# A fused attention and convolution kernel: the mask products of the first scores moved ahead of the first convolution, and one more step taken into TensorE's inner loop

## The chip, the cores and the metric

The kernel runs on one core of one Trainium2 chip. The metric is the device time of one execution in microseconds (us); a program's time is the median of its runs. Before the change it is 2295.17 us, the median of 3 runs that lie between 2292.28 and 2295.76 us.

## The reference

The input is 8 images of 128 x 128 pixels with 64 channels, in float32. Every pixel attends to its 3 x 3 neighbourhood, then three 3 x 3 convolutions with ReLU follow, and a residual is added:

```python
q = x @ Q_P;  k = neighbours(x) @ K_P;  v = neighbours(x) @ V_P      # 9 neighbours of each pixel, zero outside
scores = (k . q) * mask                 # (8, 128, 128, 9)
alpha  = softmax(scores, axis=-1)
t_in   = x + sum(alpha * v)
t = relu(conv3x3(t_in, ff1) + b1)       # 64 -> 64
t = relu(conv3x3(t,    ff2) + b2)       # 64 -> 128
t = relu(conv3x3(t,    ff3) + b3)       # 128 -> 64
out = t_in + t
```

## The kernel before

**Tiling and steps.** Two images are worked on together (rows 0 to 63 and 64 to 127 of the partitions), so there are 4 pairs. A pair is cut into 16 bands of 8 rows. TensorE runs 17 steps for a pair, k = 0 to 16, 68 in all. A step computes the attention of the next band, b, and the three convolutions of bands already there; k = 15 is the one step without attention, because the next band belongs to the next pair and is fetched by k = 16. The convolutions are run as sums and differences over pairs of columns: each has four streams whose results lie in four banks (`conv_banks`), and VectorE (DVE) joins the streams again in a "middle" and an "outer" addition.

**Attention of a band.** `r_product` (L372) multiplies x by the folded query and key weights, into `mix_bank` and `proj_bank`; ScalarE (ACT) copies the result to `rq` (L639). `scores` does half of a band: four 64 x 64 products with 400 columns (L387) write the mask, 0 inside the window and a large negative number outside, into the two banks `score_banks`; then 16 products in float32, each 32 rows of two passes in the trace (L393), add the scores to it. DVE takes the maxima (`max_scores`, L756), ACT the exponentials (L627), DVE scales (`scale`, L762 and L765) to `prob`. `turn` (L405) transposes `prob` into the same `score_banks`, ACT copies it to `probt` (L644), `mix` (L420) and `v_product` (L432) finish the band, and DVE adds x (L776).

**Order on TensorE.** It is written out by hand in `step`: r_product; the inner streams of the first convolution (`conv1`, L442); the first scores; the outer streams of conv1; the four tiles of the third convolution (`conv3_tile`, L484), with turn and the second scores between them; then the second convolution (`begin2`, `go_on2`, `end2`, L500) with mix and v_product between its parts. At its beginning the inner conv1 waits until DVE has done the outer addition of the odd rows of the step before (`outer(G, k - 1, ODD, 1)`, L866), and `conv3_tile(G, k, 0)` waits until DVE has done `middle1` of this step (L832 and L833), since both use the same banks. `conv3_tile(G, k, 1)` waits for `prob` ahead of its last two taps.

**Order on DVE.** At the start of a step: outer ODD (L866), one part of the inputs of conv1 (L794), outer EVEN (L866), inputs of both halves (L789, L790; these wait for ACT's ReLU, L693), `max_scores(b, 0)` (L756), `middle1` (L832, L833), `max_scores(b, 1)`, `outer1` (L841), `scale(b, 0)`, further inputs (L794), `scale(b, 1)`.

**Loops.** TensorE runs a loop over the 4 pairs. Inside it the steps k = 0 and 1 are written out, an inner loop of 12 turns does k = 2 to 13, and k = 14, 15 and 16 are written out. The other engines have loops of their own, in which k = 14 is also written out; the change leaves those as they are. At the end of a step `await_band` waits for the next band's x and for the end of this band's attention, in all steps but k = 14.

Of the kernel before, what the change touches and what calls it, by code (L numbers as in the profile page):

```python
# [16 lines left out]
BANDS = H // BAND  # L17
# [4 lines left out]
KEYS = HALO * HALO  # L22
PATCHES = W // PATCH
GROUP = 4
# [50 lines left out]
def build(nc, x_bands, x_keys, qt2, kt, vbd, w1, w2, w3, b1, b2, b3, window, eye, eye16, out):  # L75
    with ExitStack() as ctx:
# [3 lines left out]
        def pb(name, shape):  # L80
            return ctx.enter_context(nc.psum_tensor(name, shape, F32))
# [50 lines left out]
        for slots in (2, 2, 4, 4):  # L132
            n = slots * 3 * 128
# [7 lines left out]
        score_banks = pb("score_banks", [128, 2, 512])  # L141
# [75 lines left out]
        def outer_read(G, which, behind=0):  # L217
            n = {CONV1: 2, CONV3: 4, ODD: 7, EVEN: 8}[which]
            return G * DVE_READS + (n + DVE_READS - DVE_READS * behind - (2 if G is ALL_STEPS else 0))
# [137 lines left out]
        def _(pe):  # L357
            def hold(bank):

                nc.tensor.matmul(bank[:, 0:2], eye16_sb[:], window_sb[:, 0:2], start=True, stop=True)  # L360

            def await_band(b):
                pe.wait_ge(t_ready, b * 2)
                pe.wait_ge(xc_in, b * 16 + 16)
                pe.wait_ge(xs_in, b * 32 + 32)

            def r_product(b):
                near, far = xc[:, 1:1 + BAND, 1:65], xs[:]
                for bank, band, done, swap in ((mix_bank, near, r_done[0], False), (proj_bank, far, r_done[1], True)):
                    for rows in (LOWER, UPPER):  # L370
                        to = (UPPER if rows is LOWER else LOWER) if swap else rows
                        nc.tensor.matmul(bank[to].rearrange("c (a r s) -> c a r s", r=PATCH, s=PATCH), qk[rows],  # L372
                                         band[rows].rearrange("c r (a s) -> c a r s", s=PATCH),
                                         start=True, stop=True).then_inc(done, 1)

            def await_r(b, half):
                pe.wait_ge(r_ready, b * 2 + (half + 1))
                if half:
                    pe.wait_ge(probt_ready, b * 2 + 1)

            def scores(b, half):
                banks = [score_banks[:, n, 0:GROUP * KEYS].rearrange("q (a n) -> q a n", n=KEYS) for n in range(2)]
                mask = window_sb[:].rearrange("q (o n) -> q o n", o=1).broadcast_to([128, GROUP, KEYS])
                for n, swap in ((0, False), (1, True)):
                    for rows in (LOWER, UPPER):
                        to = (UPPER if rows is LOWER else LOWER) if swap else rows
                        nc.tensor.matmul(banks[n][to], eye16_sb[rows, rows], mask[rows], start=True, stop=False)  # L387
                for a in range(GROUP):
                    for n, swap in ((0, False), (1, True)):
                        patch = half * HALF + n * GROUP + a  # L390
                        for rows in (LOWER, UPPER):
                            to = (UPPER if rows is LOWER else LOWER) if swap else rows
                            mm = nc.tensor.matmul(banks[n][to, a], rq[rows, patch],  # L393
                                                  xc[rows, :, patch * PATCH:patch * PATCH + HALO],
                                                  start=False, stop=a == GROUP - 1)
                            if a == GROUP - 1:
                                mm.then_inc(scores_done, 1)
# [26 lines left out]
            def await_y(b):  # L424
                pe.wait_ge(y_ready, b * 2 + 2)
# [22 lines left out]
            def conv1(G, k, b, outer, att=False):  # L448


                pe.wait_ge(dt_done, b * 2 - (0 if outer else 1))
                if outer:
                    pe.wait_ge(dve_read, outer_read(G, EVEN, 1))
                else:
                    pe.wait_ge(t_kept, G * 16 + 16)
                    pe.wait_ge(dve_read, outer_read(G, ODD, 1))
                streams = (0, 3) if outer else (2, 1)
                for n, m in enumerate(streams):
                    for i in range(2):
                        if att and n == 1 and i == 1:  # L460
                            await_r(b, 0)
                        for o in ((0,) if k == BANDS else (0, 1)):
                            tap1(k, i, m, n, FULL, o, 1 if k == 0 else o, n == 0, n == 1 and k == BANDS)
                for n, m in enumerate(streams):
                    for i, rows, o in ((0, LOWER, 0), (0, UPPER, 1), (1, UPPER, 0), (1, LOWER, 1)):
                        if o == 0 and k == 0:
                            tap1(k, i, m, n, FULL, o, 0, False, n == 1)
                        elif o == 1 or k < BANDS:
                            tap1(k, i, m, n, rows, o, 1 - o, n == 0 and k == BANDS, n == 1)
# [28 lines left out]
            def tap2(k, which, j, rows, s, w, d, start, stop):  # L498
                lo, hi = pairs2(k)
                return nc.tensor.matmul(conv_banks[:, bank_of(which, j), lo * 128:hi * 128],  # L500
                                        w[rows, STREAMS[j], 2 * (which == EVEN) + s],
                                        d[rows, lo + s:hi + s, STREAMS[j]], start=start, stop=stop)
# [30 lines left out]
            def end2(G, k, j, ahead=None):  # L533

                pe.wait_ge(half_done, G * 8 + (2 * j + 2))
                for n, (w, d) in enumerate(((w2h, duh), (w2l, duh), (w2h, dul))):
                    if ahead and n == 2:
                        ahead()
                    odd = tap2(k, ODD, j, LOWER, 1, w, d, False, n == 2)
                    even = tap2(k, EVEN, j, UPPER, 0, w, d, False, n == 2)  # L540
                odd.then_inc(tile_done, 1)
                even.then_inc(tile_done, 1)
# [7 lines left out]
            r_product(0)  # L550
            await_r(0, 0)
            hold(score_banks[:, 0])
            scores(0, 0)
            await_prob(0, 0)
            hold(score_banks[:, 0])
            turn(0, 0)
            await_r(0, 1)
            hold(score_banks[:, 0])
            scores(0, 1)
            mix(0, 0)  # L560
            await_prob(0, 1)
# [11 lines left out]
            def step(G, k, b, att):  # L573
                if att:
                    r_product(b)
                conv1(G, k, b, False, att)
                if att:
                    scores(b, 0)
                conv1(G, k, b, True)
                conv3_tile(G, k, 0)  # L580
                conv3_tile(G, k, 1, (lambda: await_prob(b, 0)) if att else None)
                if att:
                    turn(b, 0)
                conv3_tile(G, k, 2, (lambda: await_r(b, 1)) if att else None)
                if att:
                    scores(b, 1)
                conv3_tile(G, k, 3)
                if att:
                    mix(b, 0)
                begin2(G, k, 0)  # L590
                go_on2(G, k, 0)
                begin2(G, k, 1, (lambda: await_prob(b, 1)) if att else None)
                if att:
                    turn(b, 1)
                go_on2(G, k, 1)
                end2(G, k, 0)
                end2(G, k, 1)
                if att:
                    mix(b, 1)
                begin2(G, k, 2, (lambda: await_y(b)) if att else None)  # L600
                if att:
                    v_product(b)
                go_on2(G, k, 2)
                begin2(G, k, 3)
                go_on2(G, k, 3)
                end2(G, k, 2)
                next_band = None if k == BANDS - 2 else b if k == BANDS - 1 else b + 1
                end2(G, k, 3, None if next_band is None else lambda: await_band(next_band))

            with pe.Fori(0, PAIRS) as p:  # L610
                g0, b0 = p * STEPS, p * BANDS
                step(g0, 0, b0 + 1, True)
                step(g0 + 1, 1, b0 + 2, True)
                with pe.Fori(0, BANDS - 4) as h:
                    step(g0 + h + 2, 2, b0 + h + 3, True)
                step(g0 + (BANDS - 2), BANDS - 2, b0 + (BANDS - 1), True)
                step(g0 + (BANDS - 1), BANDS - 1, b0 + BANDS, False)
                step(g0 + BANDS, BANDS, b0 + BANDS, True)
            for j in range(4):
# [432 lines left out]
```

## Time and profile before

| | before |
|---|---|
| median of 3 runs | 2295.17 us |
| the profiled execution, whole time | 2292.98 us |
| its span, first to last instruction | 2291.0 us |
| PE busy (TensorE matmul) | 2184.0 us, 95% |
| PEld busy (TensorE weight load) | 1222.3 us, 53% |
| DVE busy | 1894.3 us, 83% |
| ACT busy | 1132.7 us, 49% |
| mean granted TensorE clock | 0.987 of full speed |

The profiled execution is 0.1% shorter than the median. Its time is the span and 2.0 us around it. A busy PE is read with care: the ends of matmuls are modelled, and a matmul's row is longer than the slot that it takes in a stream, so slots are read from start to start.

### The profile page before, as it was taken

The numbers are of one execution on the slowest core, as the hardware profiler recorded it, in microseconds if no ns is written. First come the engines' busy times: TensorE is split into PE (matmuls) and PEld (weight loads), VectorE is DVE, ScalarE is ACT, GpSimd is POOL, SyncE is SP. The second block draws the span as 40 slices with busy tenths as digits, with TensorE's granted clock in tenths as the row PEclk, the third lists the DMA queues.
The fourth block names the chain that finished last, engine by engine and source line by source line (L and its number), as shares of the span: only waits on it lengthen the run. The fifth ranks groups of instructions, "written<-read, shape, count | busy, mean of one in ns | idle before, by whom it ended". The sixth has DMA issues, their size and how long they took to land.

```text
span 2291.0 us, 63881 instructions
## 1 busy us (share of the span) xinstructions
PE 2184.0 (95%) x24401; PEld 1222.3 (53%) x24401; DVE 1894.3 (83%) x2850; ACT 1132.7 (49%) x3108; POOL 15.5 (1%) x24
## 2 busy tenths in 40 slices
PE   4999999999899999999989999999988999999998
PEld 2555555554455555555455555555545555555554
DVE  4888888888688888888768888888876888888885
ACT  2555455553455455455345555555434555554542
POOL 2000000000000000000000000000000000000000
PEclk8999999999999999999999999999999999999999
DMA  5454544554355444544345445445534544454444
GB/s 130 140 145 142 166 141 136 155 153 136 103 155 168 145 140 147 161 145 132 118 145 154 136 154 156 145 132 166 151 117 111 168 146 142 139 166 145 141 147 124
DMA packets 291284, 328.75 MB, mean 144 GB/s; under 512 B 89300, under 2 KB 223252, under 8 KB 284564
## 3 DMA queue, kind: packets, MB, share of 16 engines
q1 hardware_dynamic: 291164, 327.17, 48.2%
q8 instruction: 73, 1.20, 0.2%
q14 instruction: 47, 0.39, 0.1%
HBM read 152.50 MB, written 33.82 MB: 81 GB/s over the span
## 4 chain that ended last, share of the span: by engine, by line
PE 87%; DVE 6%; issue 3%; ACT 1%; DMA 1%; SPq 1%; DVEq 0%; ACTq 0%
PE conv_banks L484 29%; PE conv_banks L500 24%; PE conv_banks L442 17%; PE mix_bank L420 5%; PE score_banks L393 4%; DVE work L866 3%; PE score_banks L405 3%; PE mix_bank L432 3%; PE score_banks L387 1%; DMA work<-w 1%; ACT probt L644 1%; DVE prob L765 0%; PE mix_bank L372 0%; ACT prob L627 0%; DVE tf L776 0%
## 5 line engine op out<-in xcount | busy, mean ns | idle before, releaser
L484 PE MATMUL conv_banks<-dodd,w3f 128*64 128x512 f32 (+1 forms) x1656 | 503.5, 582 | 11.9 <-DVE work L833 9.2
L484 PE MATMUL conv_banks<-deven,w3f 128*64 128x512 f32 (+1 forms) x1656 | 496.3, 570 | 8.7 <-DVE prob L765 7.0
L627 ACT ACTIVATE prob<-score_banks,negmax 128x100 f32<-128x100 f32 x1040 | 343.0, 343 | 195.4 <-DVE negmax L756 195.4
L442 PE MATMUL conv_banks<-dt,w1f 128*64 128x256 f32 (+3 forms) x4224 | 413.9, 384 | 22.3 <-DVE work L866 22.3
L442 PEld LDWEIGHTS conv_banks<-dt,w1f 128*64 128x64 f32 (+1 forms) x4224 | 219.2, 135 | 235.9 <-DVE work L866 83.4
L500 PE MATMUL conv_banks<-duh,w2h 64*128 64x512 f32 (+2 forms) x1632 | 327.6, 399 | 4.0 <-ACT m_sb L663 2.1
L500 PE MATMUL conv_banks<-duh,w2l 64*128 64x512 f32 (+2 forms) x1632 | 319.3, 388 | 6.0 <-DVE prob L765 5.2
L500 PE MATMUL conv_banks<-dul,w2h 64*128 64x512 f32 (+2 forms) x1632 | 282.4, 396 | 0.9 <-DVE tf L776 0.9
L484 PEld LDWEIGHTS conv_banks<-dodd,w3f 128*64 128x64 f32 x1656 | 138.0, 137 | 236.4 <-issue 212.0
L644 ACT COPY probt<-score_banks 100x1024 f32<-100x1024 f32 x130 | 131.8, 1014 | 235.0 <-PE score_banks L405 235.0
L484 PEld LDWEIGHTS conv_banks<-deven,w3f 128*64 128x64 f32 x1656 | 155.1, 138 | 158.8 <-issue 114.6
L639 ACT COPY rq<-mix_bank 128x512 f32<-128x512 f32 x65 | 38.2, 587 | 391.1 <-PE mix_bank L372 391.1
L756 DVE TENSOR_REDUCE negmax<-score_banks 128x4 f32<-128x400 f32 x260 | 148.5, 572 | 97.1 <-PE score_banks L393 96.5
L627 ACT ACTIVATION_READ_ACCUMULATOR prob<-score_banks,negmax 128x1 f32 x1040 | 212.2, 204 | 0.0
L693 ACT ACTIVATE relued<-work,bias 128x1024 f32<-128x1024 f32 (+2 forms) x136 | 149.6, 1103 | 92.5 <-DVE work L866 92.5
L866 DVE TENSOR_TENSOR work<-conv_banks,work 128x1024 f32<-128x1024 f32 (+2 forms) x136 | 157.5, 1163 | 44.0 <-PE conv_banks L500 44.0
L500 PEld LDWEIGHTS conv_banks<-dul,w2h 64*128 64x128 f32 x1632 | 143.5, 185 | 75.2 <-issue 53.4
L663 ACT COPY m_sb<-conv_banks 128x512 f32<-128x512 f32 (+3 forms) x205 | 108.1, 562 | 146.0 <-PE conv_banks L484 107.2
L500 PEld LDWEIGHTS conv_banks<-duh,w2l 64*128 64x128 f32 x1632 | 153.6, 185 | 49.8 <-ACT rq L634 15.1
L500 PEld LDWEIGHTS conv_banks<-duh,w2h 64*128 64x128 f32 x1632 | 153.2, 184 | 47.5 <-ACT m_sb L663 3.9
L420 PEld LDWEIGHTS mix_bank<-probt,xk 100*64 100x64 f32 x4160 | 139.4, 139 | 58.0 <-issue 56.8
L806 DVE TENSOR_TENSOR dul<-work,duh 128x1024 fp32r<-128x1024 f32 (+1 forms) x136 | 159.1, 1170 | 0.0
(93 smaller groups left out, 2937.6 us busy)
## 6 DMA issues: line engine op xcount, KB each, us to landing
xk<-x_keys SPq DMA_DIRECT2D x66, 800.0 KB
xc<-x_bands SPq DMA_DIRECT2D x66, 650.0 KB, 5.0
dodd<-dodd SPq DMA_DIRECT2D x68, 512.0 KB, 5.1
xr<-x_bands SPq DMA_DIRECT2D x264, 128.0 KB, 3.5
out<-work SPq DMA_DIRECT2D x60, 512.0 KB, 2.7
dt<-dt SPq DMA_DIRECT2D x68, 256.0 KB, 2.3
deven<-deven SPq DMA_DIRECT2D x68, 256.0 KB, 5.6
duh<-duh SPq DMA_DIRECT2D x68, 256.0 KB, 2.4
```

Of the source, the lines that this page charges most:

```text
L393: mm = nc.tensor.matmul(banks[n][to, a], rq[rows, patch], xc[rows, :, patch * PATCH:patch * PATCH + HALO], start=False, stop=a == GROUP - 1)
L420: last = nc.tensor.matmul(mix_bank[image, a * C:(a + 1) * C], xk[:, patch, image], probt[:, half, i if a < GROUP else 1 - i, a], start=Tru ...
L442: mm = nc.tensor.matmul(bank[(LOWER, UPPER)[o], n * 256 + lo * 64:n * 256 + hi * 64], w1f[i][rows, m, s, o * C:o * C + C], dt[rows, lo + s ...
L484: return nc.tensor.matmul(bank[rows, lo * 128:hi * 128], w3f[:, m, s, odd * C:odd * C + C], source[:, lo + s // 2:hi + s // 2, m], start=s ...
L500: return nc.tensor.matmul(conv_banks[:, bank_of(which, j), lo * 128:hi * 128], w[rows, STREAMS[j], 2 * (which == EVEN) + s], d[rows, lo + ...
L627: last = nc.scalar.activation(prob[:, g % 2, a], score_banks[:, g % 2, a * KEYS:(a + 1) * KEYS], ACT.Exp, bias=negmax[:, g % 2, a:a + 1], ...
L644: nc.scalar.copy(probt[:, half], score_banks[0:KEYS].rearrange("n i (a q) -> n i a q", q=C)).then_inc(probt_ready, 1)
L663: nc.scalar.copy(m2_sb[:, which % 2, lo:hi], bank[:, lo:hi]).then_inc(act_read, 1)
L693: nc.scalar.activation(to[:, lo:hi, :, 1:1 + W], sums[which][:, lo:hi], ACT.Relu, bias=bias[:, 1:2]).then_inc(relu_done, 1)
L756: nc.vector.tensor_reduce(negmax[:, g % 2], score_banks[:, g % 2, 0:GROUP * KEYS].rearrange("q (a n) -> q a n", n=KEYS), AX_X, ALU.max, ne ...
L806: nc.vector.tensor_tensor(dul[:, 1:n + 1, streams], du[:, 0:n, streams], duh[:, 1:n + 1, streams].bitcast(F32), ALU.subtract).then_inc(du_ ...
L866: nc.vector.tensor_tensor(both, m03, both, ALU.add).then_inc(dve_read, 1)
```

## The change

The four mask products leave `scores` and become a function of their own, `masks`. For the second half of a band `masks()` is called right ahead of `scores(b, 1)`, where the products were. For the first half it is called between `r_product(b)` and the inner conv1; `scores(b, 0)` stays behind the inner conv1. In the work ahead of the loops `masks()` stands right ahead of both scores. The inner loop of TensorE runs 13 turns in place of 12 (k = 2 to 14), the written-out step k = 14 goes, and with it the exception by which that step didn't wait for the next band.

```diff
-            def scores(b, half):
-                banks = [score_banks[:, n, 0:GROUP * KEYS].rearrange("q (a n) -> q a n", n=KEYS) for n in range(2)]
+            banks = [score_banks[:, n, 0:GROUP * KEYS].rearrange("q (a n) -> q a n", n=KEYS) for n in range(2)]
+
+            def masks():
                 mask = window_sb[:].rearrange("q (o n) -> q o n", o=1).broadcast_to([128, GROUP, KEYS])
                 for n, swap in ((0, False), (1, True)):
                     for rows in (LOWER, UPPER):
                         to = (UPPER if rows is LOWER else LOWER) if swap else rows
                         nc.tensor.matmul(banks[n][to], eye16_sb[rows, rows], mask[rows], start=True, stop=False)
+
+            def scores(b, half):
...
             def step(G, k, b, att):
                 if att:
                     r_product(b)
+                    masks()
                 conv1(G, k, b, False, att)
                 if att:
                     scores(b, 0)
...
                 conv3_tile(G, k, 2, (lambda: await_r(b, 1)) if att else None)
                 if att:
+                    masks()
                     scores(b, 1)
...
-                next_band = None if k == BANDS - 2 else b if k == BANDS - 1 else b + 1
-                end2(G, k, 3, None if next_band is None else lambda: await_band(next_band))
+                end2(G, k, 3, lambda: await_band(b + 1 if att else b))
...
-                with pe.Fori(0, BANDS - 4) as h:
+                with pe.Fori(0, BANDS - 3) as h:
                     step(g0 + h + 2, 2, b0 + h + 3, True)
-                step(g0 + (BANDS - 2), BANDS - 2, b0 + (BANDS - 1), True)
```

## Rows read from the trace of the kernel before

**Rows 1.** The page's part 4: the chain that ended last, by engine.

```profile
PE 87%; DVE 6%; issue 3%; ACT 1%; DMA 1%; SPq 1%; DVEq 0%; ACTq 0%
```

**Rows 2.** Waits from 112.9 to 509.6 us (k = 2 to 13): us in total, times, longest.

```profile
DVE negmax L756 <- PE score_banks L393: 11.2, 12, 0.9
...
PE conv_banks L442 <- DVE work L866: 3.4, 12, 0.3
```

**Rows 3.** Window of step k = 7: length; busy PE, PEld, DVE, ACT, POOL; clock; DMA.

```profile
311.26:344.31 33.05, 32.77 (x371) 18.14 (x369) 28.85 (x42) 17.26 (x47) 0.00 (x0) 1.00 0.49 147
```

**Rows 4.** Timeline, start of step k = 7: start, us, engine, line, operation, [idle before <-releaser].

```profile
311.46 1.23 DVE L866 TENSOR_TENSOR work<-conv_banks,work 128x1024 f32<-128x1024 f32 x1 [0.58 <-PE conv_banks L500]
311.80 0.66 PE L372 MATMUL mix_bank<-xc,qk 64*64 64x512 f32 x2
...
312.74 2.97 PE L442 MATMUL conv_banks<-dt,w1f 128*64 128x256 f32 x32 [0.28 <-DVE work L866]
```

**Rows 5.** Timeline, same step: the mask products and what stands around them.

```profile
315.32 0.13 PEld L387 LDWEIGHTS score_banks<-window_sb,eye_sb 64*64 64x64 bf16 x4
...
315.54 0.35 PE L387 MATMUL score_banks<-window_sb,eye_sb 64*64 64x400 bf16 x4
...
315.70 0.87 PE L393 MATMUL score_banks<-xc,rq 64*64 64x100 f32 x32
```

**Rows 6.** Timeline, same step: DVE's maxima and middle1, and conv3's first load.

```profile
317.43 0.55 DVE L756 TENSOR_REDUCE negmax<-score_banks 128x4 f32<-128x400 f32 x1
...
318.51 0.67 DVE L833 TENSOR_TENSOR work<-conv_banks,m_sb 128x512 f32<-128x512 f32 x1
...
319.41 0.20 PEld L484 LDWEIGHTS conv_banks<-dodd,w3f 128*64 128x64 f32 x4 [0.39 <-issue]
```

**Rows 7.** Timeline, k = 15: its start, middle1, conv3's load; k = 16: the latter two.

```profile
544.12 1.08 PE L442 MATMUL conv_banks<-dt,w1f 128*64 128x256 f32 x8 [1.41 <-DVE work L866]
...
549.38 0.68 DVE L833 TENSOR_TENSOR work<-conv_banks,m_sb 128x512 f32<-128x512 f32 x1
...
550.19 0.20 PEld L484 LDWEIGHTS conv_banks<-dodd,w3f 128*64 128x64 f32 x4 [0.65 <-issue]
...
577.04 0.28 DVE L833 TENSOR_TENSOR work<-conv_banks,m_sb 128x128 f32<-128x128 f32 x1
...
577.46 0.65 PE L484 MATMUL conv_banks<-dodd,w3f 128*64 128x512 f32 x2 [2.08 <-DVE work L833]
```

**Rows 8.** Timeline, k = 7: second maxima, outer1, and the load that awaits prob.

```profile
319.11 0.55 DVE L756 TENSOR_REDUCE negmax<-score_banks 128x4 f32<-128x400 f32 x1
319.71 1.23 DVE L841 TENSOR_TENSOR work<-conv_banks,work 128x1024 f32<-128x1024 f32 x1
...
323.52 0.38 PEld L484 LDWEIGHTS conv_banks<-deven,w3f 128*64 128x64 f32 x4 [0.48 <-DVE prob L765]
```

**Rows 9.** Timeline, step k = 1: middle1, conv3's first product, outer1, the wait for prob.

```profile
89.40 0.69 DVE L833 TENSOR_TENSOR work<-conv_banks,m_sb 128x512 f32<-128x512 f32 x1
...
90.80 1.23 DVE L841 TENSOR_TENSOR work<-conv_banks,work 128x1024 f32<-128x1024 f32 x1 [0.23 <-PE conv_banks L442]
...
90.50 0.86 PE L484 MATMUL conv_banks<-dodd,w3f 128*64 128x256 f32 x5
...
94.61 0.65 PE L484 MATMUL conv_banks<-deven,w3f 128*64 128x256 f32 x4 [1.44 <-DVE prob L765]
```

**Rows 10.** Timeline, the turns from k = 13 to the written-out k = 14.

```profile
509.27 0.40 PE L500 MATMUL conv_banks<-dul,w2h 64*128 64x512 f32 x2
509.59 0.70 PE L372 MATMUL mix_bank<-xc,qk 64*64 64x512 f32 x2
```

**Rows 11.** Timeline, the turns from one pair to the next (k = 16 to k = 0).

```profile
604.00 1.12 PE L372 MATMUL mix_bank<-xc,qk 64*64 64x512 f32 x2 [3.94 <-issue]
...
1723.03 1.11 PE L372 MATMUL mix_bank<-xc,qk 64*64 64x512 f32 x2 [6.64 <-issue]
```

**Rows 12.** Window, 6.7 us from the first turn of a pair: length, busy, clock.

```profile
601.00:607.70 6.70, 3.70 (x18) 1.36 (x20) 3.90 (x9) 2.29 (x5) 0.00 (x0) 0.50 0.50 122
```

More of the change, by code:

```diff
@@ L575, in step @@
                     r_product(b)
+                    masks()
                 conv1(G, k, b, False, att)
@@ L585, in step @@
                 if att:
+                    masks()
                     scores(b, 1)
```

## The prediction

> **What bounds the kernel now.** I read the chain of waits by engine first: TensorE is 87% of it, DVE 6% [rows 1]. The DVE part has one place. In the wait table of twelve ordinary steps TensorE's matmuls idle for one thing only, conv1 behind DVE's outer addition L866, 0.28 us in each step [rows 2, 4]. The windows say the same from outside: step k = 7 lasts 33.05 us with PE busy for 32.77 [rows 3]. Then the timeline of that step's start. The last products of the step before release DVE's outer addition at 311.46, which ends at 312.69; conv1 starts at 312.74. r_product's last row ends at 312.46, so the gap is 0.28 us [rows 4]. The end of the gap is set by DVE and not by what TensorE does in it. An ordinary step is thus a ring: TensorE's end, one DVE addition of 1.23 us, TensorE again.
>
> **Moving the masks: what it takes away.** In step k = 7 the four mask products start at 315.54 and the scores at 315.70: a slot of 0.16 us in a stream without idle time [rows 5]. Without them the scores start 0.16 us after conv1's start sooner. The first score weights must then be loaded where the mask's are now, at 315.32 during conv1's last pass, 0.22 us ahead of the slot; four loads took 0.13 us together [rows 5]. That cover holds; if it didn't, at most the 0.13 us would come back.
>
> **What it adds.** The same 0.16 us goes in behind r_product. From the end of its last row to conv1 there are 0.28 us [rows 4], and that end is modelled late, so the masks fit with at least 0.12 us to spare. r_product itself doesn't move, nor does ACT's copy of it. No wait is added: the banks' last reader was ACT's copy of the turned probabilities of the step before, for which mix has already waited. If the cover were gone, conv1 would start later by what juts out and the scores sooner by the same 0.16 us; the move would be even.
>
> **What is late next.** Here the naive sum (60 steps by 0.16 us) breaks. Behind conv1 stands conv3, which waits for middle1. DVE's way there starts at the same outer addition that releases conv1: outer, inputs, outer, inputs, maxima, middle1, one behind the other, and in k = 7 it runs from 311.46 to 319.18 (318.51 and 0.67) without pause worth naming [rows 4, 6]. The maxima start at 317.43, long after the scores' last products are issued (315.70 and 0.87 end at 316.57) [rows 5, 6]: scores that come sooner don't move them. So DVE stays where it is against the step's start, and the question is how close conv3 stands behind middle1. In k = 7 its first load is at 319.41, 0.23 us after middle1's end [rows 6]. Where conv3 really waits for middle1, the load comes 0.13 us after it: in k = 15 550.06 to 550.19, in k = 16 577.32 to 577.46 for the matmul, with 2.08 us of idle time named after L833 [rows 7]. So conv3 can come forward by 0.23 - 0.13 = 0.10 us and no more; of the 0.16 us, 0.06 turn into idle time ahead of conv3. The rows' rounding leaves 0.08 to 0.12.
>
> **Behind that gate.** The next is the wait for prob in conv3's second tile: the weight load stood 0.48 us for it while the matmuls never did [rows 8]. outer1 (L841) started at 319.71, 0.05 us after the end of the maxima before it (319.11 and 0.55) [rows 8], while middle1 and the maxima overlap by 0.07 [rows 6, 8]; I read that as a wait for conv1's end, which now comes 0.16 us sooner. I take it forward by about 0.1 us, the probabilities behind it too, so they keep pace with TensorE's 0.10. If outer1 doesn't move, the load has the time from 323.52 to its matmul's turn, some 0.2 us, which 0.10 doesn't use up. At the second scores DVE waits for TensorE again, 0.9 us in each step [rows 2], and from there to the end everything moves together.
>
> **The sum over steps.** k = 2 to 14: 13 steps by 4 pairs by 0.10 us = 5.2 us (4.2 to 6.2). k = 1: conv3 starts 0.41 us after middle1 (90.09 to 90.50), so the gate leaves 0.28; later it idles 1.44 us for prob, but the chain of prob hangs on outer1, which waited 0.23 us for conv1 [rows 9]: the whole 0.16 us goes through, 4 by 0.16 = 0.6 us. k = 16: idle for middle1 already, 2.08 us [rows 7], which DVE alone sets: nothing. k = 0: conv1 doesn't wait for DVE there; the masks are only done earlier: nothing. k = 15 has none. The second scores' masks stay where they were: nothing. Sum: 5.8 us less.
>
> **One more step in the loop.** The instructions of k = 14 are those of k = 2. A turn of the inner loop costs no more than going on to written-out code: from the last product of k = 13 to k = 14's r_product there are 0.32 us [rows 10], and k = 7, reached by the loop, shows no idle time at its start either [rows 4]. The new wait for the next band in k = 14 has queued behind it the last six products and k = 15; the other ordinary steps have that wait and never idle for it [rows 2], and the loads it names are issued in k = 14 as in them. I cost both at nothing; the bound above is the next paragraph's.
>
> **The turn of the outer loop** is different. Between pairs TensorE stands 3.94 us, once 6.64, for nothing that the profile names [rows 11], and then runs at 0.50 of the clock, 1.2 GHz, for a while [rows 12]. The program of a pair becomes a step shorter, yet the jump still goes far back. I leave these three stalls as they are, and take their own difference, 6.64 - 3.94 = 2.7 us, as what can fall out either way. The Trainium skill ("Runtime: NRT & Kernel Launch", section on instruction fetch mechanics) says that a taken branch whose target isn't among the instructions held forces a fetch before execution goes on. By that rule the stall at the outer turn stays, and the trace agrees, with 3.94 us there against none at the inner one.
>
> **Against the median.** The profiled execution took 2292.98 us, the median is 2295.17; the sum shortens either alike. 2295.17 - 5.8 = 2289.4 us (for the profiled execution 2287.2). A measurement of this kernel can tell 0.2% from no change, 4.6 us, and the forecast stands only just beyond it.
>
> **The rivals.**
> - *The gate isn't there* (12%): conv3 needs no 0.13 us behind middle1, or DVE moves too. Then 56 steps give 0.16 us, 9.0 us: 2286.2 us. Against it speaks the 0.13 us of both stalled steps [rows 7].
> - *The gate takes nearly all* (24%): DVE's chain is a little longer beside the masks, or a second gate (prob, u) stands closer than its waits show, or the scores' weights lose their cover (0.13 of 0.16 us). Each would leave 0.03 us in a step at most, 52 by 0.03 = 1.6 us: 2293.6 us. For it speaks that DVE is busy for 28.85 of 33.05 us [rows 3].
> - *The move does nothing* (5%): the masks don't fit into the gap and push conv1 by all they gave: 2295.2 us. The gap's 0.28 us speak against it.
> - *The other side* (4%): the inner loop's exit now falls into other code, and if that isn't at hand TensorE stands at each of 4 exits as at the outer turn, 3.94 us, against the 1.41 us that k = 15 waits for DVE's outer addition anyway [rows 7] and the low clock after it. It decides from the point where the stall passes that wait. With 2.5 to 3.9 us by 4 and half of a 6.7 us stretch at 0.50 clock [rows 11, 12], 4 by about 6 = 24 less 5.8: some 2313 us. The exit into k = 14 without a stall speaks against it [rows 10].
>
> The three outer turns lie across all of these: each may cost 2.7 us more or less [rows 11], and two that fall out worse take the forecast to 2289.4 + 5.4 = 2294.8 us.
>
> **How the numbers follow.** The forecast, 0.10 us in an ordinary step, has 55%. Its own size goes from 4.8 to 6.8 us, and the outer turns add about 2.7 us on either side: 2285.7 to 2293. The range for 8 in 10 takes in the missing gate and most of the second rival: 2284.5 to 2295.0. Faster by over 0.2% is below 2290.6: the 12% and four fifths of the 55%, with a little of the rest, 0.58. Slower by over 0.2% are the 4% and a trifle of the turns, 0.05. The rest, 0.37, is within.
>
> **What would show it.** In an ordinary step: L387's first four between L372 and L442, conv1 0.28 us after r_product's row as before and now with the masks' row in the gap; scores 2.80 us after conv1's start in place of 2.96; the load of conv3 0.13 us after L833's end in place of 0.23, and a new wait of L484 for L833 in all steps; a step of 32.95 us. k = 16 unchanged. Wrong would be: conv1 later than 0.05 us after L866's end (masks don't fit), a step of 32.89 us (no gate), matmuls idle for L765 (the second gate), or idle time at the start of k = 15 beyond 1.4 us.

## The result, and the profile after the change

The changed kernel takes 2281.57 us, the median of 6 runs, against 2293.73 us of the kernel before (6 runs): 12.2 us or 0.5% less, a ratio of 0.9949 with a 95% interval of 0.9937 to 0.9961. A second set of five runs gave 2281.85 us. The forecast was 5.8 us less, 2289.4 us with a range of 2284.5 to 2295.0: the direction came true, the size did not, and the time lies below the range. Of the 7.8 us between forecast and result 1.4 are the starting point, since the kernel before had 2295.17 us in its first three runs and has 2293.73 in six.

The page of the changed kernel, its span, busy times and the chain by engine (answering rows 1):

```profile
span 2278.5 us, 63905 instructions
...
PE 2183.9 (96%) x24401; PEld 1226.9 (54%) x24401; DVE 1888.2 (83%) x2850; ACT 1132.8 (50%) x3108; POOL 15.5 (1%) x24
...
PE 86%; DVE 7%; issue 3%; ACT 2%; DMA 1%; SPq 1%; DVEq 0%; ACTq 0%
```

PE is as busy as before (2184.0 us), with the same 24401 matmul rows: nothing was saved in work. What went is idle time and low clock. The timeline of step k = 7, without ACT and SP (answering rows 4, 5 and 6; the masks are now L388, conv1 L445, scores L396, conv3 L487, middle1 L838):

```profile
311.65 1.23 DVE L871 TENSOR_TENSOR work<-conv_banks,work 128x1024 f32<-128x1024 f32 x1 [0.57 <-PE conv_banks L503]
...
311.99 0.66 PE L372 MATMUL mix_bank<-xc,qk 64*64 64x512 f32 x2
312.37 0.45 PE L388 MATMUL score_banks<-window_sb,eye_sb 64*64 64x400 bf16 x4
...
312.93 2.97 PE L445 MATMUL conv_banks<-dt,w1f 128*64 128x256 f32 x32
...
315.72 0.87 PE L396 MATMUL score_banks<-xc,rq 64*64 64x100 f32 x32
...
318.65 0.69 DVE L838 TENSOR_TENSOR work<-conv_banks,m_sb 128x512 f32<-128x512 f32 x1
...
319.47 0.20 PEld L487 LDWEIGHTS conv_banks<-dodd,w3f 128*64 128x64 f32 x4 [0.43 <-issue]
```

The masks stand in the gap, and conv1 starts 0.05 us after the outer addition's end as before (312.88 to 312.93). The scores follow conv1's start by 2.79 us; before it was 2.96 (312.74 to 315.70 in rows 4 and 5). Then comes the gate: conv3's first load stands 0.13 us behind middle1 (319.34 to 319.47), where it stood 0.23 [rows 6], at exactly the distance that only the waiting steps k = 15 and 16 showed before [rows 7]. In all 48 steps k = 2 to 13 this distance is 0.13 us after the change, and 0.22 to 0.25 before it. The twelve steps k = 2 to 13 of the first pair, in one window before and after (columns as in rows 3):

```profile
112.92:509.59 396.67, 393.25 (x4418) 217.62 (x4416) 346.01 (x504) 207.01 (x564) 0.00 (x0) 1.00 0.50 148
```

```profile
113.85:508.97 395.12, 393.75 (x4418) 218.51 (x4416) 344.62 (x505) 207.06 (x564) 0.00 (x0) 1.00 0.50 149
```

A step takes 32.93 us in place of 33.06. Cutting both spans at the starts of the steps, as the timelines give them, tells where all of the 12.4 us between them lie:

| part of the span | before, us | after, us | difference |
|---|---|---|---|
| up to the first k = 1 | 82.4 | 83.6 | +1.1 |
| k = 1, four steps | 121.9 | 121.2 | -0.7 |
| k = 2 to 13, 48 steps | 1586.6 | 1580.8 | -5.8 |
| k = 14, four steps | 138.2 | 137.7 | -0.5 |
| k = 15, four steps | 107.1 | 107.1 | 0.0 |
| k = 16 up to the start of k = 0, three times | 105.4 | 100.3 | -5.0 |
| k = 0, three steps | 104.5 | 104.3 | -0.2 |
| the last k = 16 and the rest | 44.8 | 43.5 | -1.3 |

k = 1 to 14 give 7.0 us. The forecast had costed k = 16 and the outer turns at nothing, and there lie 6.3 us. What happens there is seen in k = 16, from the end of its wait for middle1 to its next wait in conv2: the four pairs before the change, then the four after it (the clock is the third number from the end):

```profile
577.46:592.72 15.26, 14.48 (x150) 6.75 (x150) 10.69 (x24) 8.70 (x37) 0.00 (x0) 1.00 0.24 50
1133.39:1150.34 16.95, 16.16 (x150) 7.08 (x150) 10.77 (x24) 8.66 (x37) 0.00 (x0) 0.90 0.21 53
1692.09:1709.05 16.96, 16.17 (x151) 7.18 (x151) 10.73 (x24) 8.66 (x37) 0.00 (x0) 0.90 0.21 49
2252.68:2269.65 16.97, 16.18 (x151) 7.18 (x152) 10.75 (x24) 8.66 (x37) 0.00 (x0) 0.90 0.21 50
```

```profile
576.74:592.00 15.26, 14.48 (x151) 6.75 (x151) 10.67 (x24) 8.67 (x37) 0.00 (x0) 1.00 0.24 50
1130.41:1147.36 16.95, 16.17 (x150) 7.16 (x150) 10.73 (x24) 8.65 (x37) 0.00 (x0) 0.90 0.21 50
1686.18:1701.45 15.27, 14.48 (x151) 6.76 (x151) 10.68 (x24) 8.70 (x37) 0.00 (x0) 1.00 0.22 59
2241.54:2256.80 15.26, 14.48 (x150) 6.75 (x150) 10.65 (x24) 8.66 (x37) 0.00 (x0) 1.00 0.23 54
```

The same work takes 15.26 us at full clock, and 16.96 where the clock falls to 1.2 GHz behind the 2.1 or 2.2 us of idle time: 1.7 us for each fall. The low stretch of the second pair before the change, by itself:

```profile
1133.41:1136.81 3.40, 3.40 (x8) 0.99 (x10) 3.13 (x8) 2.20 (x14) 0.00 (x0) 0.50 0.03 7
```

There are three falls before and one after. The third outer turn was 6.64 us before [rows 11] and is 3.81 after, which is the other 2.8 us. Against these stands a slower beginning (+1.1 us). So the study has two questions: is the gate what I took it for, and are the falls of the clock an effect of the change or of chance?

### The profile page after: what moved, and what is told of

Read it like the earlier page. It is cut to its first block, busy times and chain, and to the rows that moved or that the text cites. A ratio compares the mean times of both kernels' runs of the same rounds, so it can differ in the third digit from the quotient of the medians.

```text
span 2278.5 us, 63905 instructions
## 1 busy us (share of the span) xinstructions
PE 2183.9 (96%) x24401; PEld 1226.9 (54%) x24401; DVE 1888.2 (83%) x2850; ACT 1132.8 (50%) x3108; POOL 15.5 (1%) x24
## 4 chain that ended last, share of the span: by engine, by line
PE 86%; DVE 7%; issue 3%; ACT 2%; DMA 1%; SPq 1%; DVEq 0%; ACTq 0%
PE conv_banks L487 30%; PE conv_banks L503 24%; PE conv_banks L445 16%; PE mix_bank L423 5%; PE score_banks L396 4%; DVE work L871 3%; PE score_banks L408 3%; PE mix_bank L435 3%; PE score_banks L388 1%; DMA work<-w 1%; ACT probt L649 1%; DVE prob L770 0%; DVE negmax L761 0%; ACT relued L698 0%; PE mix_bank L372 0%
## 5 line engine op out<-in xcount | busy, mean ns | idle before, releaser
L487 PE MATMUL conv_banks<-dodd,w3f 128*64 128x512 f32 (+1 forms) x1656 | 500.8, 579 | 12.6 <-DVE work L838 9.8
L487 PE MATMUL conv_banks<-deven,w3f 128*64 128x512 f32 (+1 forms) x1656 | 494.7, 568 | 8.7 <-DVE prob L770 7.0
L445 PE MATMUL conv_banks<-dt,w1f 128*64 128x256 f32 (+3 forms) x4224 | 413.4, 383 | 12.2 <-DVE work L871 5.6
L445 PEld LDWEIGHTS conv_banks<-dt,w1f 128*64 128x64 f32 (+1 forms) x4224 | 219.0, 135 | 207.2 <-issue 71.2
L487 PEld LDWEIGHTS conv_banks<-dodd,w3f 128*64 128x64 f32 x1656 | 138.9, 137 | 237.6 <-issue 212.8
L487 PEld LDWEIGHTS conv_banks<-deven,w3f 128*64 128x64 f32 x1656 | 155.8, 138 | 155.2 <-issue 111.5
L871 DVE TENSOR_TENSOR work<-conv_banks,work 128x1024 f32<-128x1024 f32 (+2 forms) x136 | 157.1, 1160 | 43.6 <-PE conv_banks L503 43.6
```

What stands on the lines that cost most here:

```text
L445: mm = nc.tensor.matmul(bank[(LOWER, UPPER)[o], n * 256 + lo * 64:n * 256 + hi * 64], w1f[i][rows, m, s, o * C:o * C + C], dt[rows, lo + s ...
L487: return nc.tensor.matmul(bank[rows, lo * 128:hi * 128], w3f[:, m, s, odd * C:odd * C + C], source[:, lo + s // 2:hi + s // 2, m], start=s ...
L871: nc.vector.tensor_tensor(both, m03, both, ALU.add).then_inc(dve_read, 1)
```

## The experiments

A fall means in what follows that the window above takes 16.6 to 17 us in place of 15.26 to 15.5. The inner work of a profile, the sum of k = 1 to 14, is called the core sum; it is 1846.7 us before and 1839.7 after. The extra products of five kernels are these; nobody reads what they write:

```python
            def fill(n):
                many = window_sb[:].rearrange("q (o n) -> q o n", o=1).broadcast_to([128, GROUP, KEYS])
                to = mix_bank[:, 0:GROUP * KEYS].rearrange("q (a n) -> q a n", n=KEYS)
                for _ in range(n):
                    nc.tensor.matmul(to, eye16_sb[:], many, start=True, stop=True)
```

### The two halves of the change, apart

The masks moved alone, against the changed kernel, with the exception of k = 14 from its wait again:

```diff
-                end2(G, k, 3, lambda: await_band(b + 1 if att else b))
+                next_band = None if k == BANDS - 2 else b if k == BANDS - 1 else b + 1
+                end2(G, k, 3, None if next_band is None else lambda: await_band(next_band))
...
-                with pe.Fori(0, BANDS - 3) as h:
+                with pe.Fori(0, BANDS - 4) as h:
                     step(g0 + h + 2, 2, b0 + h + 3, True)
+                step(g0 + (BANDS - 2), BANDS - 2, b0 + (BANDS - 1), True)
```

> Only the masks are moved; the loops are as in the kernel before. Theory A (an ordinary step gains until conv3 meets middle1, and the rest of the 12 us comes from the steps k = 16 and the outer turns, which fall as the program's times fall): an ordinary step of 32.93 us, conv3's first load 0.13 us after middle1; 7.0 us less than before from k = 1 to 14, and another 0 to 5 us by what k = 16 and the outer turns do. Rival B (the shorter program of a pair is what shortens the outer turns): 7.0 us less and no more, 2286.7 us, the third outer turn at 6.6 us again.

Measured: 2283.18 us against 2292.45, ratio 0.9956 (0.9942 to 0.9969). The core sum is 1839.6 us, as after. Two of four pairs had a fall.

The loop alone, against the kernel before, is the same edit the other way; the change of the wait isn't shown again:

```diff
-                with pe.Fori(0, BANDS - 4) as h:
+                with pe.Fori(0, BANDS - 3) as h:
                     step(g0 + h + 2, 2, b0 + h + 3, True)
-                step(g0 + (BANDS - 2), BANDS - 2, b0 + (BANDS - 1), True)
```

> Only k = 14 is taken into the inner loop; the masks stay behind the inner conv1. Theory A: ordinary steps of 33.05 us and the same gaps as before; no difference from before, 2293.7 us, or one of about 3 us by how the outer turns and the low clock happen to fall. Rival B (the shorter program shortens the outer turns): some 4 to 5 us less, 2289 us, all of it between the start of k = 16 and that of k = 0.

Measured: 2291.85 us against 2292.45, ratio 1.0001 (0.9992 to 1.0010); core sum 1846.5 us, four falls of four. The loop step is worth nothing that shows beyond 2 us, as costed, and rival B is gone: the shorter program doesn't shorten the time. The gain belongs to the masks.

The kernel before, unchanged, for a second profile:

> The kernel before, unchanged, for a second profile. If the third outer turn's 6.64 us is a property of the program, it stands there again, at the same place; if it is how loads happen to fall in one execution, it is 3.9 us or falls on another turn. Likewise the low clock in k = 16, which stood in three of four pairs. Time 2293.7 us either way.

Measured: 2293.22 us. The core sum repeats to 0.3 us (1846.4); the falls are four of four. The third outer turn is 4.85 us in place of 6.64, the first two 3.70 and 3.57. So the turn differs between executions of one program, and the 2.8 us that it seemed to give are mostly chance of the one profiled execution. The falls are another matter: seven of eight pairs in two profiles.

### The gate at middle1

```diff
-                if att:
-                    max_scores(b, 0)
                 middle1(G, k)
                 if att:
+                    max_scores(b, 0)
                     max_scores(b, 1)
```

> The changed kernel with DVE's middle1 ahead of the first maxima, so that conv3 finds middle1 done some 0.55 us sooner. Theory A (middle1 is the gate that takes 0.06 us of an ordinary step's gain): conv3's first load comes again 0.30 us after conv1's last matmul's start in place of 0.36, an ordinary step takes 32.87 us, 52 by 0.06 = 3 us less than the changed kernel, and in k = 16 up to 0.5 us of the 2.2 us wait goes: 2277 us or so. Rival C (another gate stands right behind, prob above all, since its chain now starts 0.6 us later): steps of 32.93 us or more, with matmuls idle for prob (L770).

Measured: 2278.87 us against 2292.45 (ratio 0.9949, 0.9936 to 0.9963). The timeline of k = 7, middle1 and conv3's first load:

```profile
319.64 0.68 DVE L838 TENSOR_TENSOR work<-conv_banks,m_sb 128x512 f32<-128x512 f32 x1
...
320.86 0.20 PEld L487 LDWEIGHTS conv_banks<-dodd,w3f 128*64 128x64 f32 x4 [0.39 <-issue]
```

conv3 now stands 0.54 us behind middle1 (320.32 to 320.86), and its load has the 0.39 us before it again that it had before the change [rows 6]; the changed kernel shows 0.43. The mean of the 48 steps is 32.88 us against 32.93, and the core sum 1837.1 us, 2.6 us below the changed kernel's. The wait of k = 16 is 1.77 us in place of 2.24. Theory A gave 3 us for the core and 32.87; rival C, a second gate at prob, doesn't show: with prob's chain starting later, no ordinary step has matmuls idle for it. The gate is shown, and with it the 0.05 to 0.06 us that it took of each step's 0.16: from before (33.05) to here (32.88) the mean step is shorter by the whole 0.16 or 0.17.

### Falls of the clock: place or time?

First, was it the idle time of k = 16 at all? The products fill it:

```diff
                 conv1(G, k, b, True)
+                if k == BANDS:
+                    fill(11)
                 conv3_tile(G, k, 0)
```

> The kernel before with 11 idle-time products (400 columns in bf16, into mix_bank, read by nobody) ahead of conv3 in k = 16, where TensorE otherwise stands 2.1 us for middle1. Theory A (what the change gained beyond the 7.0 us of k = 1 to 14 is low clock after that idle time, which stood in 11 of 12 pairs of three profiles with the masks behind conv1, and costs 1.7 us each): no low clock there, conv3 of k = 16 not later by more than 0.05 us, and 4 by 11/12 by 1.7 = 6 us less than before, 2286.5 us. Rival D (the low clock in k = 16 isn't it): 2292.5 us.

> The changed kernel with the same 11 products in the same place. Theory A: with moved masks the low clock stood in 4 of 12 pairs, so only 4 by 1/3 by 1.7 = 2.3 us are left to win, 2279.3 us; its distance to the kernel before with the same products is then the 7.0 us of the ordinary steps and no more. Rival D: a distance of 10 to 12 us between those two kernels, as without the products.

Measured: 2293.91 us against 2294.26 for the one (ratio 0.9993, 0.9984 to 1.0002), 2286.06 us for the other (ratio 0.9955, 0.9942 to 0.9968; five runs, a sixth took 5819.16 us, for an unknown reason, and isn't counted). Neither gains; the second is 4 us above the changed kernel. conv3 isn't late by the products, and the fall behind the wait is gone in all eight pairs; but in three pairs of the kernel before with the products it comes later and is longer. Two windows of the first pair, one behind the wait and one from there over the rest of k = 16, the turn and the first microseconds of k = 0:

```profile
577.00:594.00 17.00, 16.11 (x176) 7.78 (x176) 12.38 (x29) 9.19 (x39) 0.00 (x0) 1.00 0.29 76
594.00:612.00 18.00, 13.30 (x116) 8.60 (x114) 8.26 (x18) 4.22 (x9) 0.00 (x0) 0.53 0.63 191
```

The second half of k = 16, with its small products and waits, ran at half clock, and so did the start of k = 0. Why was not settled. The distance between the two kernels is 7.9 us, near the 7.0 of theory A, but that is luck: in three pairs of the one stands this low stretch, and the other has long turns. So this pair of runs is a poor test of either theory: the filling took one cost away and brought others. The second kernel's own cost, which nobody had expected, is at the turn:

```profile
608.26 1.12 PE L378 MATMUL mix_bank<-xc,qk 64*64 64x512 f32 x2 [6.53 <-issue]
...
1165.22 1.12 PE L378 MATMUL mix_bank<-xc,qk 64*64 64x512 f32 x2 [6.37 <-issue]
```

All three turns are long (6.53, 6.37, 5.76 us), where the changed kernel has 3.64, 3.77 and 3.81. Only the products in k = 16 differ between the two programs. The kernel before with the same products has turns of 4.37, 3.88 and 3.81 us, so it isn't the products alone.

The direct test is to move the masks in k = 16 alone, or everywhere but there:

```diff
                 if att:
                     r_product(b)
-                    masks()
+                    if k < BANDS:
+                        masks()
                 conv1(G, k, b, False, att)
                 if att:
+                    if not (k < BANDS):
+                        masks()
                     scores(b, 0)
```

> The changed kernel, but in k = 16 the masks stay behind the inner conv1. Theory T (the low clock in k = 16 depends on when k = 16 comes, which the 1.8 us that a pair gained ahead of it have shifted): as the changed kernel, 281.8 above 2000, that is 2281.8 us, with the low clock behind conv3's wait in 1 or 2 of 4 pairs. Theory P (it depends on where the masks stand in k = 16 itself): 3 or 4 of 4 pairs, and some 4 us more, 2286 us.

The other is the same with `k == BANDS` in place of `k < BANDS`:

> The masks are moved in k = 16 alone; in all other steps they stay behind the inner conv1. k = 16 itself gains nothing by it, since conv3 waits for middle1 there. Theory T: as the kernel before, 2293 us, with 3 or 4 low stretches in k = 16. Theory P: 1 or 2 of 4, 4 us less, 2289 us.

Measured: with the masks behind in k = 16 alone 2283.39 us against 2295.03 (ratio 0.9948, 0.9935 to 0.9962) and one fall of four; with the masks moved in k = 16 alone 2294.32 us against 2295.03 (ratio 1.0000, 0.9991 to 1.0009) and four falls of four. The latter's four pairs:

```profile
578.24:595.21 16.97, 16.18 (x151) 7.18 (x152) 10.77 (x24) 8.66 (x37) 0.00 (x0) 0.90 0.22 51
1135.06:1151.83 16.77, 15.98 (x151) 7.08 (x152) 10.78 (x24) 8.66 (x37) 0.00 (x0) 0.91 0.20 48
1693.39:1710.36 16.97, 16.18 (x151) 7.19 (x151) 10.77 (x24) 8.66 (x37) 0.00 (x0) 0.90 0.21 52
2250.90:2267.83 16.93, 16.14 (x150) 7.11 (x151) 10.77 (x24) 8.66 (x37) 0.00 (x0) 0.90 0.21 48
```

Theory P falls: where the masks stand in k = 16 doesn't matter. What matters lies in the steps before it. There the moved masks only take time away, 1.6 us in each pair, so I gave the time back:

```diff
             def step(G, k, b, att):
+                if k == 1:
+                    fill(11)
                 if att:
                     r_product(b)
                     masks()
```

> The changed kernel with 11 products that nobody reads (1.84 us of work, all but the 0.1 us gap on the path) at the start of k = 1, so that a pair takes about as long as before the change. Their own price, by the profile's k = 1, should be 1.6 to 1.7 us in each pair, 6.6 us. Theory T: the low clock comes back to 3 or 4 of 4 pairs in k = 16, so 6.6 and some 4 us more than the changed kernel, 2292 us. Theory P: 1 or 2 of 4 pairs, and 2288.4 us.

Measured: 2297.76 us against 2295.03, so 16 us above the changed kernel, and 6 above the forecast of theory T. The start of the first k = 1, and the second outer turn:

```profile
84.81 0.34 PE L509 MATMUL conv_banks<-dul,w2h 64*128 64x384 f32 x2
85.08 2.04 PE L366 MATMUL mix_bank<-window_sb,eye_sb 128*128 128x400 bf16 x11
87.05 0.71 PE L378 MATMUL mix_bank<-xc,qk 64*64 64x512 f32 x2
...
1171.61 1.12 PE L378 MATMUL mix_bank<-xc,qk 64*64 64x512 f32 x2 [6.51 <-issue]
```

From the last product of k = 0 to r_product it takes 2.23 us, 0.27 in the changed kernel, and k = 1 is otherwise 0.07 us shorter (30.23 against 30.30): the products cost 1.9 us in each pair, 7.6 in all. And the falls are back:

```profile
580.49:597.45 16.96, 16.18 (x150) 7.17 (x150) 10.76 (x24) 8.65 (x37) 0.00 (x0) 0.90 0.20 47
1140.80:1157.76 16.96, 16.17 (x151) 7.17 (x152) 10.74 (x24) 8.66 (x37) 0.00 (x0) 0.90 0.20 46
1701.35:1718.02 16.67, 15.88 (x151) 7.09 (x152) 10.77 (x24) 8.65 (x37) 0.00 (x0) 0.91 0.21 53
2261.05:2277.76 16.71, 15.93 (x150) 7.09 (x150) 10.76 (x24) 8.65 (x37) 0.00 (x0) 0.91 0.21 46
```

Four of four, with the masks moved in every step. The count is what theory T said; the time isn't a test of it. 7.6 us and three more falls of 1.7 are 12.7, and the profile's span is 20.3 us longer than the changed kernel's: 7.4 us more lie in the three turns, 5.66, 6.51 and 6.41 us in place of 3.64, 3.77 and 3.81. They are long as in the other changed kernel with eleven products, and as unexplained. They lengthen the pairs too: from wait to wait it is 559.7 to 560.6 us here, 555.9 to 560.6 before. Theory T holds by the falls: whether the idle time of k = 16 costs one depends on when k = 16 comes. The changed kernel, unchanged, once more:

> The changed kernel unchanged, for a second profile and more runs. Ordinary steps at 32.93 us again. Theory A: the low clock in k = 16 stands in fewer than three of four pairs again, and the time is again about 11 us below before, 2281.8 us. If that was chance, 3 or 4 of 4, and 7 to 8 us below, 2285 us.

Measured: 2281.85 us against 2294.26, ratio 0.9946 (0.9934 to 0.9959), one fall of four, core sum 1840.7 us. Counted together, the four profiles whose ordinary steps are as before (the kernel before twice, the loop alone, the masks moved in k = 16 alone) have 15 falls in 16 pairs. The four whose ordinary steps are short and that have no further edit (the changed kernel twice, the masks alone, the masks behind in k = 16) have 5 in 16. Of the other kernels with short steps the one with middle1 first has one in four, and the two of the next section have three in four and one in four.

The granted clock settles it better than these counts. In each of the fourteen profiles all changes of the clock lie on one even beat: they are whole multiples of the same length apart, to 0.004 us, from the first to the last. I laid the start of each wait of k = 16 on the beat of its own profile, for the 48 pairs of the twelve profiles in which the wait isn't filled. All 29 waits with a fall start in one part of the beat and all 19 without a fall in the other; the nearest two of different kind are 0.03 us apart. This holds for either place of the masks, for waits of 1.77, 2.08 and 2.24 us and for the kernel with the delay. Where in the beat its wait comes thus tells a pair's fall, and nothing else about a pair was needed to sort the 48. Why the waits of a kernel with the old steps come nearly always in the one part was not worked out, so that the numbers 15 and 5 are counts and not a law.

### Two ways to gain more

Products behind the last one of k = 16, ahead of the outer loop's jump:

```diff
                 step(g0 + BANDS, BANDS, b0 + BANDS, True)
+                fill(14)
             for j in range(4):
```

> The changed kernel with 14 such products behind the last one of k = 16, ahead of the outer loop's jump, 2.3 us of work. If TensorE's queue holds them while its sequencer stands at the jump, they take idle time only: the turn's idle time falls from 3.7 to about 1.4 us, step k = 0 starts when it did, and the low clock behind the turn (3.4 to 6.8 us in each, half of it lost) goes in most: 3 by 1.7 to 3.4 us, 2273 to 2277 us. If the jump's fetch only begins once they are done, k = 0 starts 2.3 us later each time and nothing is won: 2288 us.

Measured: 2280.37 us against 2294.26 (ratio 0.9937, 0.9924 to 0.9950). The second turn of its profile:

```profile
1157.63 2.54 PE L366 MATMUL mix_bank<-window_sb,eye_sb 128*128 128x400 bf16 x14
1161.61 0.70 PE L378 MATMUL mix_bank<-xc,qk 64*64 64x512 f32 x2 [1.43 <-issue]
```

From the last product of k = 16 to k = 0 it takes about as long as before, with 2.54 us of it filled: the queue works on while the sequencer stands at the jump. r_product's row is 0.70 us, which was 1.12 in the turns at low clock [rows 11], and no turn of this profile is followed by a low clock. The first turn was longer here (2.74 us idle beside the 2.54), and three of four pairs fell in k = 16, since pairs come at other times again. That ate most of the gain, and the time came out between the two forecasts: 1.5 us remain, and the intervals overlap.

Both edits together:

> The two edits that won over the changed kernel together: DVE's middle1 ahead of the first maxima, and 14 products behind k = 16 to keep TensorE at work during the turn of the outer loop. Ordinary steps at 32.88 us, no low clock behind the turns: between the 2278.9 of the one and 1.5 to 6 us less, 2275 us.

Measured: 2275.58 us against 2295.03, ratio 0.9915 (0.9901 to 0.9929), the best of all: 6 us below the changed kernel. Its profile has one fall in four pairs, and behind none of the turns does the clock fall; behind the first:

```profile
604.01:610.80 6.79, 5.58 (x39) 2.55 (x39) 1.55 (x2) 1.07 (x2) 0.00 (x0) 1.00 0.53 153
```

## Why the prediction was wrong

- **The gap and the masks' price**: right. The masks fit, conv1 starts 0.05 us after L871, the scores came 0.17 us sooner against 0.16 forecast.
- **The gate at middle1**: right, and the reordering of DVE showed it. It lets 0.12 us of 0.16 through in the mean of 48 steps, where I had 0.10 with 0.08 to 0.12 for the rounding. Of the difference 0.01 us is DVE's chain to middle1, shorter by that much in the mean of the first profile after the change (7.70 against 7.71 us; 7.71 in the second). I had also said that the wait would show for conv3's matmuls in every step; it doesn't, since the modelled end of conv1's last row covers it. It shows only in the distance from middle1 and in the load's 0.43 us.
- **k = 1**: 0.7 us against 0.6. **k = 15, k = 0, the loop, the new wait**: nothing, as costed.
- **The sum of the ring** was thus 7.0 us in the two profiles of before and after; between the means of five profiles of either kind (1846.7 and 1840.2 us) it is 6.5. The forecast of 5.8 us had room for that (4.8 to 6.8).
- **What failed is the term for k = 16**: "k = 16: idle for middle1 already, 2.08 us, which DVE alone sets: nothing". The idle time indeed didn't shrink (2.24 us, since the scores end sooner and middle1 doesn't). But I had read it only as a wait and not asked what the clock did behind it, though the window of the turn [rows 12] had shown me that a stand is followed by 1.2 GHz. In k = 16 the fall costs 1.7 us, stood in 15 of 16 pairs, and depends on when the step comes. The change made pairs 1.6 us shorter ahead of it, and the falls went to 5 of 16: 2.5 falls fewer in an execution, 4.3 us. That they became fewer and not more was luck as far as I can tell; nothing in my working would have given the sign. 6.5 and 4.3 are 10.8 us, of 12.2 measured (11.5 between the means of all runs of the two kernels, 2293.7 of 75 and 2282.2 of 11). The last microsecond stays open; the starts and the turns differ by more than that between executions.
- **The turns**: I had given them 2.7 us either way for one execution. That was the right size for one. As a shift between the two kinds of kernel they gave little: the three turns together take 10.9 to 14.5 us in the four profiles with the old steps and 11.0 to 12.9 in the four with the short ones.
- **The range** let the clock enter only through the turns, so its lower end stood on the rival without a gate. It should have reached down by the three falls that the profile of before held, 5.1 us.
- **The rivals**: none took place. The stall at the inner loop's exit doesn't show, k = 15 starts after 1.41 us as before.

## What to carry to other kernels

When work goes into a gap, follow the engine that ends the gap: what it does next is the limit of the gain, and the distance that a waiting step shows behind its releaser, against the distance in an ordinary step, prices that limit before anything is built. Then look through the program for idle times of some two microseconds whose following window has a lower clock in some repetitions and not in others; a small change anywhere ahead of them moves their cost, in either direction, and a forecast should hold that in its range. And two kernels are compared by the repeated inner part too: here it agreed to about 1 us between profiles of one kind, where whole executions of one program differ by up to 8 us, and of the one with the delay by 13.

## What the runs showed of the hardware

- An idle time of 1.8 to 2.2 us on TensorE was followed by a granted clock of 0.50, 1.2 GHz, in some pairs and not in others of the same execution. Between the changed kernel and the one with the delay in k = 1, falls went from 1 of 4 to 4 of 4. Filling the idle time with products took that fall away in eight pairs and brought a longer one in the second half of the step in three of them, at 0.53 of the clock over 18 us in the window shown.
- All changes of the clock in a profile lie on one even beat, and where in it the idle time starts separated 29 pairs with a fall from 19 without. The Trainium skill ("TensorE: Matmul & The Clock Gate", Part 1, on the clock gate) says that the time base by which the clock is decided runs freely and isn't reset by a kernel's start, so that the point of change varies. The trace agrees: the beat runs through each of the fourteen profiles whatever the kernel does.
- A jump back over the outer loop's whole body costs 3.4 to 4.0 us of standing in most turns, and 4.4 to 6.6 in some. Two kernels with 11 products and their loads added inside a pair had three long turns each (5.7 to 6.5 us), a third with the same addition had not (3.8 to 4.4 us). Why was not settled. The inner loop's jump costs nothing that shows.
- TensorE works off what is queued while its sequencer stands at such a jump: 14 products of 2.54 us hid in it in two turns of three, where 1.2 to 1.4 us of standing were left, and the clock stayed up behind all three.
- A load that waits for DVE started 0.05 us after DVE's end where the load itself carried the wait (conv1), and 0.13 us where another wait stood between the one for DVE and the load (conv3, in all 48 ordinary steps after the change).
